# A decoder layer's self-attention: value products in pairs of quarters, single PSUM banks for both score passes

## What is computed

```
q = x @ Wq + bq;  k = x @ Wk + bk;  v = x @ Wv + bv          # x: layernormed
scores = einsum("bghnd,bhsd->bghns", q, k)
attn   = softmax(scores / 4, axis=-1)
out    = einsum("bghns,bhsd->bghnd", attn, v)                # then @ Wo + bo
```

## Time and profile before

| | us |
|---|---|
| median of 3 executions | 2008.24 |
| lowest, highest | 1996.96, 2011.62 |
| the profiled execution | 1998.29 |
| its span in the trace | 1996.6 |
| attention's steps (first B tile to last quarter) | 155.5 to 811.6 |

### The profile page before, as it was taken

The page is one execution under the profiler, slowest core; times in us unless marked ns, Lnnn a source line. Parts: engine busy times, 40 slices in busy tenths (PEclk is TensorE's granted clock), DMA queues, the critical chain, the costliest instruction groups (busy, mean ns, idle before and its releaser), DMA issues. The chain is left out here.

```text
span 1996.6 us, 35818 instructions
## 1 busy us (share of the span) xinstructions
PE 1794.5 (90%) x11908; PEld 1177.3 (59%) x11909; DVE 1250.6 (63%) x2492; ACT 1038.1 (52%) x2238; POOL 409.4 (21%) x455
## 2 busy tenths in 40 slices
PE   6799999999999999889689999979437899999978
PEld 3443333333333333569678999968326688888857
DVE  6498999999999993242278999957114223222223
ACT  2205888888888889312367888843113233332322
POOL 3000000000000000410032222210740354544530
PEclk9957999999999999887989999989669899999999
DMA  5601221112111110351102020032003223323223
GB/s 172 176 8 27 42 35 27 26 27 47 30 27 26 34 20 3 95 171 81 56 7 69 18 71 17 24 125 96 9 10 108 43 48 53 50 50 53 48 50 113
DMA packets 86687, 109.40 MB, mean 55 GB/s; under 512 B 19564, under 2 KB 68128, under 8 KB 85504
## 3 DMA queue, kind: packets, MB, share of 16 engines
q1 hardware_dynamic: 69440, 88.12, 15.6%
q0 software_dynamic: 16032, 19.36, 5.9%
q10 hardware_dynamic: 1104, 0.43, 0.1%
HBM read 64.15 MB, written 38.48 MB: 51 GB/s over the span
## 5 line engine op out<-in xcount | busy, mean ns | idle before, releaser
L497 DVE TENSOR_REDUCE half_max<-psA 128x1 f32<-128x512 f32 x1024 | 634.3, 684 | 39.5 <-PE psA L547 39.1
L528 ACT ACTIVATE PT<-psB 128x1024 f32<-128x1024 f32 x512 | 517.9, 1026 | 167.1 <-PE psB L557 166.8
L547 PE MATMUL psA<-KS,QS 48*128 48x512 f32 x1024 | 407.8, 481 | 24.4 <-PEq L102 16.3
L557 PE MATMUL psB<-QS,KS 50*128 50x512 f32 x1024 | 364.8, 458 | 0.4 <-ACT PT L528 0.4
L576 PE MATMUL psO<-PT,VG 128*32 128x256 f32 x4096 | 330.3, 395 | 4.8 <-ACT OU L518 0.8
L547 PEld LDWEIGHTS psA<-KS,QS 48*128 48x128 f32 x1024 | 169.5, 196 | 249.4 <-DVE half_max L497 188.5
L576 PEld LDWEIGHTS psO<-PT,VG 128*32 128x32 f32 x4096 | 82.3, 108 | 191.1 <-issue 121.1
L1350 ACT ACTIVATE x_probs<-x_scores,x_neg_max 128x77 f32<-128x77 f32 x512 | 176.3, 358 | 3.7 <-DVE x_neg_max L1252 3.5
L1919 DVE TENSOR_TENSOR m_xT<-m_psT,m_xT 128x256 fp32r<-128x256 f32 x72 | 30.6, 425 | 234.6 <-ACT m_xT L1956 234.6
L557 PEld LDWEIGHTS psB<-QS,KS 50*128 50x128 f32 x1024 | 145.7, 187 | 19.8 <-ACT PT L528 17.4
L1853 POOL DMA_INDIRECT acc<-m_y,tokens x72 | 114.6, 1592 | 172.6 <-DVE m_y L1931 169.8
(11 more groups left out here) (233 smaller groups left out, 2789.8 us busy)
## 6 DMA issues: line engine op xcount, KB each, us to landing
QS<-q_parts SPq DMA_DIRECT2D x96, 128.0 KB
q_parts<-part SPq DMA_DIRECT2D x16, 512.0 KB, 2.7
OT<-OU SPq DMA_DIRECT2D x32, 256.0 KB, 2.6
KS<-k_parts SPq DMA_DIRECT2D x32, 128.0 KB
xf_rows<-XF SPq DMA_DIRECT2D x32, 128.0 KB, 1.7
acc<-X SPq DMA_DIRECT2D x32, 128.0 KB, 1.8
WG<-in_Wg SPq DMA_DIRECT2D x8, 512.0 KB, 10.0
WU<-in_Wu SPq DMA_DIRECT2D x8, 512.0 KB, 10.4
```

Of the source, the lines that this page charges most:

```text
L497: dve.tensor_reduce(half_max[:, h * TB + t, n:n + 1], psA[:, bank_of(slot, 2 * v + r), :], axis=AX.X, op=ALU.max).then_inc(max_taken, 1)
L528: act.activation(PT[:, k % 4, 2 * a:2 * a + 2, :].rearrange("p h n -> p (h n)"), psB[:, u % 2, :, :].rearrange("p a n -> p (a n)"), ACT.Ex ...
L547: pe.matmul(psA[:, bank_of(slot, m), :], QS[top:top + KQ, slot, h // 2, t * P:(t + 1) * P], KS[top:top + KQ, slot, n * HALF:(n + 1) * HALF ...
L557: mm = pe.matmul(psB[:, u % 2, r, :], KS[top:top + KM, slot, c * P:(c + 1) * P], QS[top:top + KM, slot, a, half * HALF:(half + 1) * HALF], ...
```

## The change

- `times_values` is called twice, for two quarters in succession, in each odd step, and not in even steps. The quarters are those of u - 5 and u - 4, so a quarter is used in the step it was used in before or one later.
- `psA` has four banks (RING_A), and an A tile waits for the maximum four tiles before.
- `psB` has three single banks (RING_B) in place of two pairs. Each B tile waits for the exponential of the tile three before it, and each signals its own completion.
- Each step has two 512-wide exponentials in place of one 1024-wide. ScalarE waits for each B tile. The order of the two B tiles in a step, and the place in `PT` that each goes to, are kept.

```diff
-RING = 3
+RING_A = 4
+RING_B = 3
-        psA = ctx.enter_context(nc.psum_tensor("psA", [P, RING, HALF], F32))
-        psB = ctx.enter_context(nc.psum_tensor("psB", [P, 2, 2, HALF], F32))
+        psA = ctx.enter_context(nc.psum_tensor("psA", [P, RING_A, HALF], F32))
+        psB = ctx.enter_context(nc.psum_tensor("psB", [P, RING_B, HALF], F32))
...
             def exps(i, slot):
                 for u in range(NU):
                     k, a = divmod(u, 2)
-                    act.wait_ge(b_done, count(i, NU, u + 1))
                     if a == 0 and (k >= 4 or not (isinstance(i, int) and i < 1)):
                         act.wait_ge(pv_done, count(i, NC, k - 3))
-                    act.activation(PT[:, k % 4, 2 * a:2 * a + 2, :].rearrange("p h n -> p (h n)"),
-                                   psB[:, u % 2, :, :].rearrange("p a n -> p (a n)"), ACT.Exp, scale=SCALE).then_inc(exp_done, 1)
+                    for n in range(2):
+                        act.wait_ge(b_done, count(i, 2 * NU, 2 * u + n + 1))
+                        act.activation(PT[:, k % 4, 2 * a + 1 - n, :], psB[:, bank_of(slot, 2 * u + n), :], ACT.Exp,
+                                       scale=SCALE).then_inc(exp_done, 1)
...
-                    pe.wait_ge(max_taken, count(i, 2 * NU, bank_free(slot, m)))
+                    pe.wait_ge(max_taken, count(i, 2 * NU, m - RING_A + 1))
...
-                if first and not (isinstance(i, int) and i == 0 and u < 2):
-                    pe.wait_ge(exp_done, count(i, NU, u - 1))
+                m, top = 2 * u + n, (1 - n) * ROWS
+                if not (isinstance(i, int) and i == 0 and m < RING_B):
+                    pe.wait_ge(exp_done, count(i, 2 * NU, bank_free(slot, m)))
...
                     for r in range(2):
                         if has_a:
                             pass_a(i + ahead, (slot + ahead) % SLOTS, (u + LEAD) % NU, r)
-                        pass_b(i, slot, u, 1 - r, r == 0)
-                    if u >= LAG:
-                        times_values(i, e, u - LAG)
-                    elif not (isinstance(i, int) and i < 1):
-                        times_values(i - 1, 1 - e, u - LAG + NU)
+                        pass_b(i, slot, u, r)
+                    if u % 2 == 0:
+                        continue
+                    for w in (u - LAG - 1, u - LAG):
+                        if w >= 0:
+                            times_values(i, e, w)
+                        elif not (isinstance(i, int) and i < 1):
+                            times_values(i - 1, 1 - e, w + NU)
```

More of the change, by code:

```diff
@@ L406, in bank_of @@
         def bank_of(slot, m):
-            return (slot * 2 * NU + m) % RING
+            return (slot * 2 * NU + m) % RING_B
         def bank_free(slot, m):
-            if m >= RING:
-                return m - RING + 1
+            if m >= RING_B:
+                return m - RING_B + 1
             before = (slot - 1) % SLOTS
@@ L496, in maxima @@
                         dve.wait_ge(a_done, count(i, 2 * NU, 2 * v + r + 1))
-                        dve.tensor_reduce(half_max[:, h * TB + t, n:n + 1], psA[:, bank_of(slot, 2 * v + r), :],
+                        dve.tensor_reduce(half_max[:, h * TB + t, n:n + 1], psA[:, (2 * v + r) % RING_A, :],
                                           axis=AX.X, op=ALU.max).then_inc(max_taken, 1)
@@ L519, in take_out, with exps @@
                                ACT.Copy).then_inc(out_copied, 1)
-            def exps(i):
+            def exps(i, slot):
                 for u in range(NU):
                     k, a = divmod(u, 2)
-                    act.wait_ge(b_done, count(i, NU, u + 1))
                     if a == 0 and (k >= 4 or not (isinstance(i, int) and i < 1)):
                         act.wait_ge(pv_done, count(i, NC, k - 3))
-                    act.activation(PT[:, k % 4, 2 * a:2 * a + 2, :].rearrange("p h n -> p (h n)"),
-                                   psB[:, u % 2, :, :].rearrange("p a n -> p (a n)"), ACT.Exp, scale=SCALE).then_inc(exp_done, 1)
+                    for n in range(2):
+                        act.wait_ge(b_done, count(i, 2 * NU, 2 * u + n + 1))
+                        act.activation(PT[:, k % 4, 2 * a + 1 - n, :], psB[:, bank_of(slot, 2 * u + n), :], ACT.Exp,
+                                       scale=SCALE).then_inc(exp_done, 1)
                     if u == LAG - 2 and not (isinstance(i, int) and i < 1):
@@ L535, in _ @@
             for i in range(NG):
-                exps(i)
+                exps(i, i % SLOTS)
             take_out(NG - 1, 1)
@@ L543, in pass_a, with pass_b @@
                 m, top = 2 * v + r, r * ROWS
-                if not (isinstance(i, int) and i == 0 and m < RING):
-                    pe.wait_ge(max_taken, count(i, 2 * NU, bank_free(slot, m)))
-                pe.matmul(psA[:, bank_of(slot, m), :], QS[top:top + KQ, slot, h // 2, t * P:(t + 1) * P],
+                if not (isinstance(i, int) and i == 0 and m < RING_A):
+                    pe.wait_ge(max_taken, count(i, 2 * NU, m - RING_A + 1))
+                pe.matmul(psA[:, m % RING_A, :], QS[top:top + KQ, slot, h // 2, t * P:(t + 1) * P],
                           KS[top:top + KQ, slot, n * HALF:(n + 1) * HALF], start=True, stop=True).then_inc(a_done, 1)
-            def pass_b(i, slot, u, r, first):
+            def pass_b(i, slot, u, n):
                 k, a = divmod(u, 2)
                 half, c = divmod(k, TB)
-                top = r * ROWS
-                if first and not (isinstance(i, int) and i == 0 and u < 2):
-                    pe.wait_ge(exp_done, count(i, NU, u - 1))
[L557 to L560, removed]
+                m, top = 2 * u + n, (1 - n) * ROWS
+                if not (isinstance(i, int) and i == 0 and m < RING_B):
+                    pe.wait_ge(exp_done, count(i, 2 * NU, bank_free(slot, m)))
+                pe.matmul(psB[:, bank_of(slot, m), :], KS[top:top + KM, slot, c * P:(c + 1) * P],
+                          QS[top:top + KM, slot, a, half * HALF:(half + 1) * HALF], start=True, stop=True).then_inc(b_done, 1)
             def times_values(i, e, w):
@@ L566, in times_values @@
                 if q == 0:
-                    pe.wait_ge(exp_done, count(i, NU, 2 * k + 2))
+                    pe.wait_ge(exp_done, count(i, 2 * NU, 4 * k + 4))
                 if c == 0 and q == 0:
```

## The result

The change made the kernel slower. Its median is 2112.5 us (4 runs) against 2002.6 us (4 runs); the ratio is 1.055, with a 95% interval of 1.050 to 1.060. The forecast was 2062 us. The sign and the place were right, and 60 of the 110 us were foreseen. The profiled execution took 2104.65 us, 106 more than that of before.

The account below looks back on a forecast made before the run. TensorE was taken to bound the kernel, VectorE close behind. Steps with A +28, without A +13, psO copies +19 and +1, maxima's rows -3, slot wraps +1: together +59 us, giving 2062 us, range 2022 to 2100.

Parts of the forecast that it names:

- TensorE leads, VectorE is close behind: Attention steps with A tiles before the change: TensorE sets 1.24 us a step, VectorE has 0.042 us to spare.
- The saving by pairs of quarters: Values on TensorE: a pair takes 1.00 us in place of 1.14, gaining 0.14 us every two steps.
- psA with four banks costs nothing: A tiles' bursts of four: costed at nothing; up to 1.00 us if the fourth bank were missing.
- The loop over three banks for B: Each burst's fourth B tile waits for the first one's bank: two steps take 2.60 us, against 2.48 with A, 1.99 without.
- B0 to the exponential's start: From the start of a burst's first B tile until ScalarE begins its exponential: 0.54 us of the two-step period.
- The exponential and its release: The 512-wide exponential, 0.60 us, then 0.04 us until TensorE may reuse the B bank.
- take_out: Copy of psO on ScalarE, exponentials queued behind: 1.11 us each, in place of 0.44 with A tiles, 0.72 without.
- The first steps unchanged: The 11 steps of the first group at the 1.2 GHz level stay at 2.16 us each, bounds -3 and 0 us.
- The clock: Rival: new waits drop TensorE's clock in a tenth of the step pairs, +40 us, 2102 us; chance 0.06.
- What the profile would show: Expected trace: 2.6 us period, steps without A 1.30 us, VectorE's share 0.92, ScalarE's near 0.8, exponentials near 598 ns.

Follow-up runs that it names:

- rings_b4a3: The changed kernel with three banks for A tiles and four for B; paired quarters and 512-wide exponentials stay; ratio 1.0225 to the kernel before.
- before_paired: The kernel before with only the quarters of values paired; three banks for A, two pairs for B, 1024-wide exponentials; ratio 1.0265.
- half_exp: The changed kernel with exponentials over 256 of each tile's 512 columns, the other half of PT constant; ratio 1.007 to the kernel before.
- single: The changed kernel with one quarter of values a step again; its banks and 512-wide exponentials stay; ratio 1.018 to the kernel before.
- late_take: The changed kernel with each copy of psO one step later in ScalarE's order; ratio 1.036 to the kernel before.
- before_turn1: The kernel before with TURN_AT 1 in place of 4, so VectorE turns the maxima's parts three steps sooner; ratio 0.9955.
- pairs_b4a3: Against the kernel before: three banks for A, four for B, 512-wide exponentials, later psO copies, a quarter of values after every two tiles; ratio 1.000.
- late_tail_single: The changed kernel with psO copies one step later and single quarters in the 42 steps without A tiles; ratio 1.016 to the kernel before.
- triples_b4a3: Against the kernel before: values after every three A/B tile pairs, three banks for A, four for B, 512-wide exponentials, later psO copies; ratio 0.9951.

## Why the prediction was right in kind and short in size

- *TensorE leads, VectorE is close behind*: right. With all loops gone the time moved by 1% only, to VectorE's pace.
- *The saving by pairs of quarters*: right. A pair of quarters took 1.00 us up to the next tile, as worked out.
- *psA with four banks costs nothing*: right; with three (`rings_b4a3`, `before_paired`) it would have been the same loop on VectorE.
- *The loop over three banks for B*: right in mechanism (`half_exp`, `single`), 2.71 us in place of 2.60. The term that was mis-sized is B0 to the exponential's start: 0.62 us, not 0.54. The 0.54 came from the earlier trace rows, where ScalarE went from one exponential to the next and started 0.04 us after the tile's end. Here it waited for the tile, and its start came 0.12 us after the tile's end. The exponential and its release took 0.65, not 0.64. 0.11 us in 224 periods is 25 us, the largest part of what was missing besides the clock.
- *take_out*: 3.69 us from values to values where 3.72 was worked out, so 0.98 us above the longer period where the sum had 1.11; right. The place was shown by `late_take`.
- *The first steps unchanged*: the clock rose 15 us sooner (at 165 and not 180 us) and they took 5 us less. That this is the change's doing isn't shown: in `before_turn1` it rose at 167 us, in `pairs_b4a3` at 184.
- *The clock*: this step failed. It stood among the rivals, with a chance of 0.06, as something that would come in place of the forecast. It came on top of it, with 36 us. The argument against it was that the steps without A wait in each step and stay at 1.00. But there TensorE's matmuls covered 41.87 of 43 us: what waited was the weight load, under a matmul that still ran. The new waits leave no matmul running, for 0.52 us in every 2.66 without A tiles and for 0.53 us at once behind a take_out, and the clock's falls went with them (`late_take`, `late_tail_single`). Why it fell at these waits and not at the longer ones of `before_paired` stays open. The page "TensorE: Matmul & The Clock Gate" of the Trainium skill, section "A second HAM failure mode: psum-queue depth-cycling", describes such a swing, from short idle times between groups of matmuls. It was cited with no row that showed it; the trace of the changed kernel agrees, with nine falls in the 14 groups, seven groups over 46 us and the last 57 us at the lower level. That of `before_paired` doesn't: more time without a matmul, and no fall.
- *What the profile would show*: B3 starts 1.27 us after B0 (1.17 worked out), and a step without A tiles takes 1.33 us (1.30) until the clock falls. VectorE's share is 0.86 (0.92) and ScalarE's 0.73 (near 0.8), both lower as the groups took longer than worked out.

Together: 59 us forecast, +36 clock, +25 loop, -4 take_outs, -5 first steps, -5 that before lost by itself make 106, as measured.

## What to carry over

When consumers' tiles are issued in bursts, compare the burst with the ring of banks first. A tile that needs the bank of a tile in its own burst puts a whole produce, consume and release time into every period, whatever the engines' loads are. Cheaper switches are worth having only as far as the rings are at least as long as the bursts. And if the remedy puts new waits on TensorE, price a fall of the clock into the sum, not beside it: here it was worth 36 us, while the waits of `before_paired` cost nothing in clock, so the trace has to tell.

## What the runs showed of the hardware

- ScalarE's exponential on 128x512 lasts 0.605 us, on 128x256 0.384, on 128x1024 1.026; four of 512 columns in succession take 2.06 us.
- ScalarE, waiting for a tile, started 0.07 us or 0.13 us after the tile's end as the profile has it, and how long it had been idle doesn't decide which. In the kernel before it was mostly 0.07 us with 0.2 to 0.9 us idle, as in the earlier trace rows; in `single` 0.13 us with 0.2 to 1.1 us idle (119 times in 400 to 760 us); in `triples_b4a3` mostly 0.07 us with 0.2 to 0.7 us idle. What decides stays open.
- TensorE's granted clock fell to 1.2 GHz after three waits of 0.52 us without a matmul, 2.68 us apart (`late_take`), but stayed at 2.4 GHz through seven waits of 0.51 us, 2.67 us apart (the changed kernel), with 0.30 us in every 2.46 (`half_exp`) or 0.32 us in every 2.71 (`rings_b4a3`), and with 71 of 540 us without a matmul (`before_paired`).
- Once fallen, it stayed at 1.2 GHz for 27 us in `pairs_b4a3` while matmuls covered all of that time, and for 58 us at the end of the changed kernel, where 0.32 us without a matmul came in every 4.12.
